# Where the FFN's output halves are summed, and when ScalarE scales the residual, in a linear-attention and FFN layer

## The chip, the cores and the metric

The kernel runs on one core of a Trainium2 chip. The metric is the device time of one execution in microseconds (us); lower is better.

## The reference

One transformer layer in fp32 on x of shape (32, 512, 256): a causal linear attention with 16 heads of 16 on the normalised x, and an FFN with quantised weights on the layer-normed result. Both add to a residual; the reference normalises twice ahead of the FFN (once outside, once inside it).

```
x = x + attn(layernorm(x))          # phi(q), phi(k) = elu+1; causal linear attention; @ Wo.T + bo
x = x + ffn(layernorm(x))           # ffn(r) = r + 0.5 * (silu(layernorm(r)*gamma+beta @ w1 + b1) @ w2 + b2)
```

So the output is x1 + layernorm(x1) + 0.5 z + 0.5 b2, where x1 is the attention's output with its residual and z the second matmul of the FFN. x1 + layernorm(x1) is x1 times a number per token plus a number per token: the kernel's `res_mul` and `res_add`.

## The kernel before

A batch is 512 tokens of 256 features: C = 4 chunks of 128 tokens, T = 2 halves of 128 features. Every engine has a program of its own, written out by hand, and engines wait for each other through counters (`Event`): `w.need(event, shift, k)` waits until the k-th count of the batch `i + shift` is there, `event.done(instruction)` counts. An engine runs its program strictly in the order written. SP issues the DMAs from one queue.

A pass `i` of the loop (`pe_iteration`, `ve_iteration`, `ac_iteration`, `po_iteration`, `sp_iteration`) works on three batches at once: the attention of batch i, the FFN of batch i-1, and the normalisation and the q and k projections of batch i+1. There are 33 passes, the first without an FFN, the last with the FFN alone.

TensorE's pass, in order: the v projection (`project_v`), transposes of k (`kt`) and of the normed x1 (`ht0`, `ht1`), 16 small matmuls for the denominators, then the first FFN matmul in eight blocks j, each in two halves `f{j}a` and `f{j}b` (`fc1(j)`, L356/L357), interleaved with the attention's scores (L400) and values (L437) of eight units u; then the transposes of the next batch's x (`ident,x_hat`, L331), q and k projections, the second FFN matmul `fc2` of chunks 0 and 1, the output projection `wo`, and `fc2` of chunks 2 and 3. Three PSUM banks go round in a ring: `f3b` takes the bank of `f2a`, and so waits until ScalarE has read `f2a` in `ffn_scaled(2)`.

ScalarE's pass (`ac_iteration`), in order: a Silu on one column, for its table (`table_warm`); four copies of v into `v_pad`, after the v projection; two copies `k_tok`; two scaled copies `gt_hi` from `ht0`, `ht1`; `ffn_scaled(0)` and `ffn_scaled(1)` (L757, they read `f0a`, `f1a`); four `res` copies (L829); `ffn_silu(0)` (L765 and L768); `ffn_scaled(2)`; then the other blocks, and at the end the exponentials of the next batch through the tile `clip` (L794, L797).

`res` is one tile of [128, 4, 256]. ScalarE writes res = x1 * res_mul + res_add into it (L829), GpSimd adds the bias (L919), VectorE adds half of `z` in two halves, in place (`final`, L644), and SP stores each half from it (`sp_store`, L965). So L829 of the next pass waits for the stores of this one:

```
w.need(res_c, -1)
w.need(store, -2)
for c in range(C):
    last = e.activation(res[:, c, :], x1[:, c, :], ACT.Identity, ...)
```

SP's pass: the load of x for batch i+2, then for each t the q and k rows of batch i+1 out to DRAM and back as stacked operands (L943 to L955), the store of half 0, the second load of x (`xb`, L938), the store of half 1.

VectorE's pass ends with `final(0)`, a scan, the sum `x1` (L713), its statistics, the normed `x_hat` (L730), `res_mul` (L732), `res_add` (L733, event `res_c`), and `final(1)`; the next pass begins with `gt_lo` (L655), which `fc1(0)` waits for.

Of the kernel before, what the change touches and what calls it, by code (L numbers as in the profile page):

```python
# [26 lines left out]
ALU = mybir.AluOpType  # L27
ACT = mybir.ActivationFunctionType
# [45 lines left out]
def build(nc, x, wq_t, bq, wk_t, bk, wv_t, bv, wo_t, bo, gamma, beta, q1, sc1, b1, q2, sc2, b2, out):  # L74
# [4 lines left out]
    C = S // P  # L79
# [13 lines left out]
    out_v = out.rearrange("b (c p) d -> b p c d", p=P)  # L93

    with ExitStack() as ctx:
        def sb(name, shape, dtype=F32):
            return ctx.enter_context(nc.sbuf_tensor(name, shape, dtype))
# [4 lines left out]
        def sem(name):  # L102
            return ctx.enter_context(nc.semaphore(name))
# [29 lines left out]
        clip = sb("clip", [P, 2, S])  # L133
# [10 lines left out]
        x1 = sb("x1", [P, C, D])  # L144
        hn2 = x_hat
        res = sb("res", [P, C, D])
# [8 lines left out]
        res_mul, res_add = sb("res_mul", [P, C]), sb("res_add", [P, C])  # L155
# [29 lines left out]
        def qk_bank(is_q, m):  # L185

            return sc[is_q] if m else ring_bank("kq"[is_q] + "0")
# [7 lines left out]
        def ring_bank(use):  # L195
            return BORROWED[use] if use in BORROWED else ring[RING[use]]


        def ev(name, per, **more):
            return Event(sem(name), per, **more)  # L200
# [35 lines left out]
        res_c = ev("res_c", 1)  # L236
        x_again = ev("x_again", 1, step=16)
        e_hn2 = ev("e_hn2", C)
        F_ = dict(early=1)
        res_m, e_res = ev("res_m", 1, **F_), ev("e_res", 1, **F_)  # L240
        ht_pe, ht_h, ht_l = ev("ht_pe", T, **F_), ev("ht_h", T, **F_), ev("ht_l", T, **F_)
        f_pe = ev("f_pe", T * FT, **F_)
        f_a, f_b = ev("f_a", FT, **F_), ev("f_b", FT, **F_)
# [1 line left out]
        z_pe, e_out = ev("z_pe", C // 2, **F_), ev("e_out", C // 2, **F_)  # L245
        store = ev("store", 2, step=16, **F_)
# [315 lines left out]
        def ve_iteration(e, i, A, Fn, N, preparation=(None, None, None)):  # L562

            w = Waiter(e, i)
# [74 lines left out]
            def final(n):  # L639

                w.need(z_pe, -1, n)
                w.need(e_res, -1)
                cs = slice(2 * n, 2 * n + 2)
                e_out.done(e.scalar_tensor_tensor(  # L644
                    out=res[:, cs, :], in0=ring_bank(f"z{n}")[:, :].rearrange("p (c d) -> p c d", c=2), scalar=0.5,
                    in1=res[:, cs, :], op0=ALU.mult, op1=ALU.add))

            if N:
                ve_norm_x(e, w, 1)
# [2 lines left out]
            if Fn:  # L652
                for t in range(T):
                    w.need(ht_h, -1, t)
                    ht_l.done(e.scalar_tensor_tensor(  # L655
                        out=gt_lo[:, t, :], in0=ring_bank(f"ht{t}")[:, :], scalar=gamma_c[:, t:t + 1],
                        in1=gt_hi[:, t, :].bitcast(F32), op0=ALU.mult, op1=ALU.subtract))
# [46 lines left out]
            if Fn:  # L704
                final(0)
            if N:
                cumulate(1, 1)
            if A:
                w.need(e_xb)
                for n in range(2):  # L710
                    w.need(wo_pe, 0, n)
                    cs = slice(2 * n, 2 * n + 2)
# [4 lines left out]
                for c in range(C):  # L717
                    last = e.bn_stats(stats2[:, c, :], x1[:, c, :])
                ln2_st.done(last)
                w.alone(ln2_st, 0)  # L720
                for c in range(C):
                    last = e.bn_aggr(mv2[:, c, :], stats2[:, c, :])
# [6 lines left out]
                for c in range(C):  # L729
# [4 lines left out]
                                                  op0=ALU.mult, op1=ALU.mult))  # L734
            if Fn:
                final(1)


        def ac_iteration(e, i, A, Fn, N):
            w = Waiter(e, i)  # L740
# [5 lines left out]
            def ffn_scaled(j):  # L746

                if not Fn:
                    return
                w.need(f_pe, -1, T * j)  # L750
                if j >= SLOTS:
                    w.need(sl, -1, j - SLOTS)
                elif A:
                    w.need(k_out[j % T], 0)
                else:
                    w.need(sl, -2)
                f_a.done(e.activation(silu_f[:, j % SLOTS, :], ring_bank(f"f{j}a")[:, :], ACT.Identity,  # L757
                                      bias=bias_1[:, j:j + 1], scale=scale_1[:, 0, j:j + 1]))

            def ffn_silu(j):  # L760
                if not Fn:
                    return
                slot = silu_f[:, j % SLOTS, :]
                w.need(f_b, -1, j)
                silu.done(e.activation(slot, slot, ACT.Silu))  # L765
                w.need(silu, -1, j)
                w.need(z_pe, -2)
                sh.done(e.activation(s_hi[:, j, :], slot, ACT.Copy))  # L768
# [15 lines left out]
            def exponentials(t, s):  # L784
                for n in (2 * t, 2 * t + 1):
                    m, is_q = n // 2, n % 2
                    w.need(qk_pe, s, n)
                    if n >= 2:
                        w.need(phi, s, n - 2)
                    else:  # L790
                        w.need(phi, s - 1)

                    part = clip[:, n % 2, :]
                    qk_clip.done(e.activation(part, qk_bank(is_q, m)[:, :], ACT.Relu,  # L794
                                              bias=bias_qkm[:, 1 - is_q, m:m + 1], scale=-1.0))
                    w.need(qk_clip, s, n)
                    qk_exp.done(e.activation(part, part, ACT.Exp, scale=-1.0))  # L797

            if Fn:
                e.activation(table_warm[:, 0:1], ones[:, 0:1], ACT.Silu)  # L800
            if A:
                for c in range(C):
                    w.need(v_pe, 0, c // 2)
                    if c == 0:
                        w.need(av_pe, -1)
                    h = c % 2
                    v_sb.done(e.activation(  # L807
                        v_pad[:, c, :, 0:4:3, :],
                        ring_bank(f"v{c // 2}")[:, h * D:(h + 1) * D].rearrange("p (r a x) -> p r a x", a=2, x=HD),
                        ACT.Copy))  # L810
            if A:
                for n in range(2):
                    w.need(kt_pe, 0, n)
                    w.need(upd_pe, -1)
                    kt_sb.done(e.activation(k_tok[:, 2 * n:2 * n + 2, :],
                                            ring_bank(f"kt{n}")[:, :].rearrange("p (c d) -> p c d", c=2), ACT.Copy))
            if Fn:
                for t in range(T):
# [3 lines left out]
                                           scale=gamma_c[:, t:t + 1]))  # L822
            ffn_scaled(0)
            ffn_scaled(1)
            if Fn:
                w.need(res_c, -1)
                w.need(store, -2)
                for c in range(C):
                    last = e.activation(res[:, c, :], x1[:, c, :], ACT.Identity, bias=res_add[:, c:c + 1],  # L829
                                        scale=res_mul[:, c:c + 1])  # L830
                res_m.done(last)
            ffn_silu(0)
            ffn_scaled(2)
            if A:
# [39 lines left out]
            if N:  # L874

                e.activation(table_warm[:, 0:1], ones[:, 0:1], ACT.Exp)  # L876
                exponentials(0, 1)
# [54 lines left out]
        def sp_load(e, w, s, batch):  # L932
            w.need(xhat, s - 1)
            load.done(e.dma_start(x_in[:, :, :], x_v[batch]))

        def sp_load_again(e, w, s, batch):
            w.need(e_x1, s - 1)
            x_again.done(e.dma_start(xb[:, :, :], x_v[batch]))  # L938

        def sp_stack(e, w, t, s):  # L940
            w.need(e_kl, s, t)
            for n, part in enumerate((k_hi, k_lo)):
                e.dma_start(k_rows[t, n], part[:, t, :]).then_inc(k_out[t].sem, 16)  # L943
            w.need(e_ql, s, t)
            for n, part in enumerate((q_hi, q_lo)):
                e.dma_start(q_rows[t, n], part[:, t, :]).then_inc(q_out[t].sem, 16)
            w.need(k_out[t], s)
            for n, part in enumerate((0, 1, 0)):
                e.dma_start(k_stack[2 * HD * n:2 * HD * (n + 1), t, :, :].bitcast(F32),
                            k_rows[t, part].rearrange("(g r) n -> r g n", g=PAIRS)).then_inc(k_in[t].sem, 16)  # L950
            w.need(q_out[t], s)
            for n, part in enumerate((0, 0, 1)):
                for odd in range(2):
                    first = HD * (2 * n + odd)
                    e.dma_start(q_stack[first:first + HD, t, :, odd, :].bitcast(F32),  # L955
                                q_rows[t, part].rearrange("(g a r) n -> a r g n", g=PAIRS, a=2)[odd])\
                        .then_inc(q_in[t].sem, 16)

        def sp_iteration(e, i, A, Fn, N, N2):
            w = Waiter(e, i)  # L960

            def sp_store(n):
                w.need(e_out, -1, n)
                cs = slice(2 * n, 2 * n + 2)
                store.done(e.dma_start(out_v[i - 1][:, cs, :], res[:, cs, :]))  # L965

            if N2:
                sp_load(e, w, 2, i + 2)
            if N:
                for t in range(T):  # L970
                    sp_stack(e, w, t, 1)
            if Fn:
                sp_store(0)
            if N:
                sp_load_again(e, w, 1, i + 1)
            if Fn:
                sp_store(1)
# [202 lines left out]
```

## Time and profile before

| | |
|---|---|
| median of 3 runs (lowest to highest) | 1870.67 us (1870.02 to 1875.25) |
| the profiled execution: its own time, its span | 1868.04 us, 1866.3 us |
| busy share: TensorE, weight loads, VectorE, ScalarE, GpSimd | 90%, 78%, 66%, 63%, 44% |
| mean granted TensorE clock | 0.935 of 2.4 GHz |
| DMA traffic | 222.86 MB, mean 119 GB/s |

The span is the stretch between the first and the last instruction of the profiled execution; the execution's own time is 1.74 us more. The busy share of TensorE counts time at either clock.

### The profile page before, as it was taken

The numbers are of one execution on the slowest core, as the hardware profiler recorded it, in microseconds if no ns is written. First come the engines' busy times: TensorE is split into PE (matmuls) and PEld (weight loads), VectorE is DVE, ScalarE is ACT, GpSimd is POOL, SyncE is SP. The second block draws the span as 40 slices with busy tenths as digits, with TensorE's granted clock in tenths as the row PEclk, the third lists the DMA queues.
The fourth block names the chain that finished last, engine by engine and source line by source line (L and its number), as shares of the span: only waits on it lengthen the run. The fifth ranks groups of instructions, "written<-read, shape, count | busy, mean of one in ns | idle before, by whom it ended". The sixth has DMA issues, their size and how long they took to land.

```text
span 1866.3 us, 39341 instructions
## 1 busy us (share of the span) xinstructions
PE 1686.4 (90%) x13860; PEld 1460.0 (78%) x13860; DVE 1240.0 (66%) x2513; ACT 1174.8 (63%) x2020; POOL 829.9 (44%) x594
## 2 busy tenths in 40 slices
PE   3998889999999888999999999998999989899987
PEld 3787778877888777888777888877878877778776
DVE  5776677666677666677666677666677666677652
ACT  2476556676665675666676665676665776566653
POOL 3254334544434544344544434544334544335543
PEclk8898999999999998999999999999999999999988
DMA  6743665334555335555334555334555334655320
GB/s 167 161 115 94 146 146 143 90 94 111 146 146 137 95 97 110 146 146 127 105 94 112 146 146 146 94 97 101 146 146 140 97 93 108 146 146 123 88 65 17
DMA packets 153937, 222.86 MB, mean 119 GB/s; under 512 B 20032, under 2 KB 71488, under 8 KB 153920
## 3 DMA queue, kind: packets, MB, share of 16 engines
q1 hardware_dynamic: 149152, 222.36, 47.4%
q10 hardware_dynamic: 4768, 0.28, 0.2%
q8 instruction: 10, 0.16, 0.0%
q14 instruction: 7, 0.06, 0.0%
HBM read 138.69 MB, written 83.89 MB: 119 GB/s over the span
## 4 chain that ended last, share of the span: by engine, by line
DMA 26%; PE 26%; ACT 14%; SPq 13%; DVE 10%; issue 9%; ACTq 1%; DVEq 0%; POOL 0%; POOLq 0%
DMA out<-res 12%; DMA k_rows<-silu_f 10%; SPq L955 8%; PE ring L301 5%; DMA q_rows<-probs 5%; PE ring L356 5%; PE sc L400 4%; PE num L437 4%; PE ring L357 3%; ACT res L829 3%; ACT silu_f L757 3%; PE ring L459 2%; DVE probs L531 2%; ACT L876 2%; ACT silu_f L765 2%
## 5 line engine op out<-in xcount | busy, mean ns | idle before, releaser
L902 POOL TENSOR_TENSOR s_lo<-silu_f,s_hi 128x512 fp32r<-128x512 f32 x256 | 340.1, 1334 | 472.8 <-ACT s_hi L768 472.8
L604 DVE SCALAR_TENSOR_TENSOR silu_f<-ring,scale,silu_f 128x512 f32<-128x512 f32 x224 | 168.3, 751 | 358.8 <-ACT silu_f L757 343.1
L356 PE MATMUL ring<-gt_hi,w_q 128*128 128x512 f32 x448 | 217.3, 485 | 109.3 <-ACT silu_f L757 109.1
L301 PE MATMUL ring<-w_hi,s_hi 128*128 128x256 f32 x1024 | 291.8, 285 | 6.4 <-POOL s_lo L902 4.9
L301 PE MATMUL ring<-w_lo,s_hi 128*128 128x256 f32 x1024 | 291.7, 285 | 0.0
L301 PE MATMUL ring<-w_hi,s_lo 128*128 128x256 f32 x1024 | 291.6, 285 | 0.0
L531 DVE TENSOR_TENSOR probs<-sc,causal 128x512 f32<-128x512 f32 x384 | 251.1, 682 | 8.8 <-PE sc L400 8.5
L356 PEld LDWEIGHTS ring<-gt_hi,w_q 128*128 128x128 f32 x448 | 92.9, 207 | 170.7 <-ACT silu_f L757 124.4
L400 PE MATMUL sc<-q_stack,k_stack 96*128 96x256 f32 x1024 | 209.0, 323 | 8.6 <-DVE probs L531 5.5
L400 PEld LDWEIGHTS sc<-q_stack,k_stack 96*128 96x128 f32 x1024 | 170.7, 212 | 44.9 <-DVE probs L531 27.8
L301 PEld LDWEIGHTS ring<-w_hi,s_hi 128*128 128x128 f32 x1024 | 198.5, 194 | 8.2 <-issue 7.0
L924 POOL TENSOR_TENSOR qk<-qk,phi_q 128x512 f32<-128x512 f32 x64 | 83.0, 1297 | 273.3 <-DVE qk L583 273.3
L301 PEld LDWEIGHTS ring<-w_lo,s_hi 128*128 128x128 f32 x1024 | 198.5, 194 | 1.2
L301 PEld LDWEIGHTS ring<-w_hi,s_lo 128*128 128x128 f32 x1024 | 198.5, 194 | 0.0
L807 ACT ACTIVATE v_pad<-state_acc 128x256 f32<-128x256 f32 x64 | 21.1, 381 | 277.4 <-PE state_acc L301 277.4
L357 PE MATMUL ring<-gt_lo,w_q 128*128 128x512 f32 x448 | 192.0, 429 | 0.0
L911 POOL TENSOR_TENSOR probs<-probs,causal 128x512 f32<-128x512 f32 x128 | 165.0, 1289 | 57.6 <-ACT probs L851 54.3
L757 ACT ACTIVATE silu_f<-ring,bias,scale 128x512 f32<-128x512 f32 x224 | 171.7, 766 | 27.0 <-PE ring L357 25.6
L437 PE MATMUL num<-probs,v_pad 128*32 128x128 f32 x4096 | 173.5, 290 | 0.4 <-DVE probs L531 0.3
L768 ACT ACTIVATE s_hi<-silu_f 128x512 fp32r<-128x512 f32 x256 | 161.8, 632 | 8.1
L765 ACT ACTIVATE silu_f<-silu_f 128x512 f32<-128x512 f32 x256 | 159.7, 624 | 0.0
L829 ACT ACTIVATE res<-x,res_add,res_mul 128x256 f32<-128x256 f32 x128 | 66.4, 589 | 112.6 <-DMA out<-res 112.6
(159 smaller groups left out, 4047.6 us busy)
## 6 DMA issues: line engine op xcount, KB each, us to landing
k_stack<-k_rows SPq DMA_DIRECT2D x192, 256.0 KB, 3.9
q_stack<-q_rows SPq DMA_DIRECT2D x384, 128.0 KB, 5.7
k_rows<-silu_f SPq DMA_DIRECT2D x128, 256.0 KB, 4.4
q_rows<-probs SPq DMA_DIRECT2D x128, 256.0 KB, 4.6
x_in<-in_x SPq DMA_DIRECT2D x32, 512.0 KB, 6.2
xb<-in_x SPq DMA_DIRECT2D x32, 512.0 KB, 7.5
out<-res SPq DMA_DIRECT2D x64, 256.0 KB, 7.1
v_pad<-in_q SPq DMA_DIRECT2D x2, 512.0 KB, 8.3
```

The source lines that it names most:

```text
L301: last = e.matmul(target, a, b, start=(n == 0), stop=(n == 3 * len(pairs) - 1))
L356: e.matmul(ring_bank(use)[:, :], w1_q[:, t, cols], gt_hi[:, t, :], start=True, stop=False)
L357: f_pe.done(e.matmul(ring_bank(use)[:, :], w1_q[:, t, cols], gt_lo[:, t, :], start=False, stop=True))
L400: last = e.matmul(sc[r][:, 2 * n * P:2 * (n + 1) * P], k_stack[:, t, pair, toks], q_stack[:, t, pair, :, toks], start=True, stop=True)
L437: last = e.matmul(num[t][32 * pair:32 * pair + 32, c * P:(c + 1) * P], v_pad[:, c, t * HT // 2 + pair, 2 * odd:2 * odd + 2, :], probs[u % ...
L531: masked[r].done(e.tensor_tensor(half_probs(u, r), sc[r][:, :].rearrange("p (h q) -> p h q", h=HV), causal[:, None, :].to_broadcast([P, HV ...
L604: f_b.done(e.scalar_tensor_tensor(out=slot, in0=ring_bank(f"f{j}b")[:, :], scalar=scale_1[:, 1, j:j + 1], in1=slot, op0=ALU.mult, op1=ALU. ...
L757: f_a.done(e.activation(silu_f[:, j % SLOTS, :], ring_bank(f"f{j}a")[:, :], ACT.Identity, bias=bias_1[:, j:j + 1], scale=scale_1[:, 0, j:j ...
L765: silu.done(e.activation(slot, slot, ACT.Silu))
L768: sh.done(e.activation(s_hi[:, j, :], slot, ACT.Copy))
L902: sl.done(e.tensor_tensor(s_lo[:, j, :], silu_f[:, j % SLOTS, :], s_hi[:, j, :].bitcast(F32), ALU.subtract))
L911: po_masked.done(e.tensor_tensor(half_probs(j, 1), half_probs(j, 1), causal[:, None, :].to_broadcast([P, HV, P]), ALU.mult))
```

## The change

`final` writes its sum to `clip`, half n to `clip[:, n, :]`, and the stores read it from there. So `final` and the first exponential of the next batch wait for the stores of the batch before, and L829 no longer does; it now needs only that `final(n)` of the batch before has read `res`. L829 becomes `residual(n)` (L807 after), two copies for each half, and moves from behind `ffn_scaled(1)` to the head of ScalarE's pass: `residual(0)` ahead of the v copies, `residual(1)` between the second and the third of them. `residual` is in the program of every pass that has an FFN.

```diff
-        res_m, e_res = ev("res_m", 1, **F_), ev("e_res", 1, **F_)
+        res_m, e_res = ev("res_m", 2, **F_), ev("e_res", 1, **F_)
...
                 w.need(z_pe, -1, n)
                 w.need(e_res, -1)
+                w.need(store, -2)
                 cs = slice(2 * n, 2 * n + 2)
                 e_out.done(e.scalar_tensor_tensor(
-                    out=res[:, cs, :], in0=ring_bank(f"z{n}")[:, :].rearrange("p (c d) -> p c d", c=2), scalar=0.5,
-                    in1=res[:, cs, :], op0=ALU.mult, op1=ALU.add))
+                    out=clip[:, n, :], in0=ring_bank(f"z{n}")[:, :], scalar=0.5,
+                    in1=res[:, cs, :].rearrange("p c d -> p (c d)"), op0=ALU.mult, op1=ALU.add))
...
                         w.need(phi, s - 1)
+                        w.need(store, s - 3)
...
+            def residual(n):
+
+                if Fn:
+                    w.need(res_c, -1)
+                    w.need(e_out, -2, n)
+                    for c in (2 * n, 2 * n + 1):
+                        last = e.activation(res[:, c, :], x1[:, c, :], ACT.Identity, bias=res_add[:, c:c + 1],
+                                            scale=res_mul[:, c:c + 1])
+                    res_m.done(last)
+
             if Fn:
                 e.activation(table_warm[:, 0:1], ones[:, 0:1], ACT.Silu)
-            if A:
-                for c in range(C):
+            residual(0)
+            for c in range(C):
+                if A:
                     w.need(v_pe, 0, c // 2)
...
+                if c == 1:
+                    residual(1)
...
             ffn_scaled(1)
-            if Fn:
-                w.need(res_c, -1)
-                w.need(store, -2)
-                for c in range(C):
-                    last = e.activation(res[:, c, :], x1[:, c, :], ACT.Identity, bias=res_add[:, c:c + 1],
-                                        scale=res_mul[:, c:c + 1])
-                res_m.done(last)
             ffn_silu(0)
...
-                store.done(e.dma_start(out_v[i - 1][:, cs, :], res[:, cs, :]))
+                store.done(e.dma_start(out_v[i - 1][:, cs, :], clip[:, n, :].rearrange("p (c d) -> p c d", c=2)))
```

The first place is ScalarE's program from the head of the loop's pass to `ffn_scaled(2)`. Before, with the events that each row waits for (`v_pe` is the v projection, `kt_pe` and `ht_pe` are the transposes, `f_pe` the first FFN matmul, `f_b` VectorE's sum of its two halves):

```order
L807 ACTIVATE v_pad<-state_acc 128x8x2x16 [waits av_pe,v_pe]
L807 ACTIVATE v_pad<-state_acc 128x8x2x16
L807 ACTIVATE v_pad<-ring 128x8x2x16 [waits v_pe]
...
L821 ACTIVATE gt_hi<-ring,gamma_c 128x512 [waits ht_pe]
L757 ACTIVATE silu_f<-num,bias,scale 128x512 [waits k_out0,f_pe]
L757 ACTIVATE silu_f<-ring,bias,scale 128x512 [waits k_out1,f_pe]
L829 ACTIVATE res<-x,res_add,res_mul 128x256 [waits store,res_c]
L829 ACTIVATE res<-x,res_add,res_mul 128x256 x3
L765 ACTIVATE silu_f<-silu_f 128x512 [waits f_b]
L768 ACTIVATE s_hi<-silu_f 128x512 [waits z_pe,silu]
L757 ACTIVATE silu_f<-ring,bias,scale 128x512 [waits f_pe]
```

The same stretch after the change:

```order
L807 ACTIVATE res<-x,res_add,res_mul 128x256 [waits e_out,res_c]
L807 ACTIVATE res<-x,res_add,res_mul 128x256
L820 ACTIVATE v_pad<-state_acc 128x8x2x16 [waits av_pe,v_pe]
L820 ACTIVATE v_pad<-state_acc 128x8x2x16
L807 ACTIVATE res<-x,res_add,res_mul 128x256 [waits e_out]
L807 ACTIVATE res<-x,res_add,res_mul 128x256
L820 ACTIVATE v_pad<-ring 128x8x2x16 [waits v_pe]
...
L758 ACTIVATE silu_f<-ring,bias,scale 128x512 [waits k_out1,f_pe]
L766 ACTIVATE silu_f<-silu_f 128x512 [waits f_b]
L769 ACTIVATE s_hi<-silu_f 128x512 [waits z_pe,silu]
L758 ACTIVATE silu_f<-ring,bias,scale 128x512 [waits f_pe]
```

The four copies and the wait for `store` have left the place between `ffn_scaled(1)` and `ffn_silu(0)`; a pair stands on either side of the first two v copies, waiting for `res_c` and `e_out`. The second place is the end of VectorE's pass, after the change, with the two `final` rows (L645), where `wo_pe` is the output projection:

```order
L71 ISA [waits e_res,z_pe]
L645 SCALAR_TENSOR_TENSOR clip<-ring,res 128x512 [waits store]
L583 SCALAR_TENSOR_TENSOR qk<-ones,phi_k 128x512 [waits phi]
L714 TENSOR_TENSOR x<-ring,xb 128x512 [waits wo_pe,e_xb]
...
L733 TENSOR_SCALAR res_mul<-ln_rstd 128x4
L734 SCALAR_TENSOR_TENSOR res_add<-mv,ln_rstd 128x4
L645 SCALAR_TENSOR_TENSOR clip<-ring,res 128x512 [waits z_pe]
```

The order there is as before; only the wait for `store` and one instruction that carries a wait are new.

## Rows read from the trace of the kernel before

**Rows 1.** The page, part 1: busy time of each engine.

```profile
PE 1686.4 (90%) x13860; PEld 1460.0 (78%) x13860; DVE 1240.0 (66%) x2513; ACT 1174.8 (63%) x2020; POOL 829.9 (44%) x594
```

**Rows 2.** Who waited for whom: us in total, times, longest us.

```profile
ACT v_pad L807 <- PE state_acc L301: 277.4, 31, 9.2
...
ACT res L829 <- DMA out<-res: 112.6, 30, 5.8
PE ring L356 <- ACT silu_f L757: 109.1, 32, 5.7
```

**Rows 3.** Timeline of ACT, one pass: start us, us, instruction [idle before, releaser].

```profile
933.76 0.66 ACT L807 ACTIVATE v_pad<-state_acc 128x256 f32<-128x256 f32 x2 [9.19 <-PE state_acc L301]
935.10 0.66 ACT L807 ACTIVATE v_pad<-ring 128x256 f32<-128x256 f32 x2 [0.69 <-PE ring L301]
...
941.09 0.78 ACT L757 ACTIVATE silu_f<-ring,bias,scale 128x512 f32<-128x512 f32 x1 [0.58 <-PE ring L357]
944.71 2.08 ACT L829 ACTIVATE res<-x,res_add,res_mul 128x256 f32<-128x256 f32 x4 [2.84 <-DMA out<-res]
946.69 0.61 ACT L765 ACTIVATE silu_f<-silu_f 128x512 f32<-128x512 f32 x1
...
947.87 0.76 ACT L757 ACTIVATE silu_f<-ring,bias,scale 128x512 f32<-128x512 f32 x1
...
969.97 0.67 ACT L794 ACTIVATE clip<-ring,bias_qkm 128x512 f32<-128x512 f32 x1
```

**Rows 4.** The chain that ended last, in the same pass.

```profile
936.65 8.03 DMA out<-res
```

**Rows 5.** Timeline of PE, the same pass.

```profile
936.65 1.85 PE L450 MATMUL state_acc<-head_one,qk 128*128 128x8 f32 x16
938.88 0.49 PE L356 MATMUL num<-gt_hi,w_q 128*128 128x512 f32 x1 [0.39 <-DVE gt_lo L655]
...
945.58 0.50 PE L356 MATMUL ring<-gt_hi,w_q 128*128 128x512 f32 x1
...
948.68 0.50 PE L356 MATMUL ring<-gt_hi,w_q 128*128 128x512 f32 x1 [2.37 <-ACT silu_f L757]
```

**Rows 6.** Stretches of the same pass; behind the busy times PEclk, DMA share, GB/s.

```profile
940.00:942.00 2.00, 2.00 (x7) 1.63 (x6) 1.28 (x4) 1.29 (x2) 0.00 (x0) 0.50 1.04 207
950.00:952.00 2.00, 2.00 (x11) 1.80 (x9) 1.35 (x4) 1.97 (x5) 1.16 (x1) 0.51 0.00 0
970.00:972.00 2.00, 2.00 (x23) 1.54 (x16) 0.66 (x1) 1.94 (x5) 2.00 (x2) 1.00 0.00 0
```

**Rows 7.** Timeline of ACT, `res` copies: the first and last between which 28 passes lie.

```profile
156.84 2.07 ACT L829 ACTIVATE res<-x,res_add,res_mul 128x256 f32<-128x256 f32 x4 [5.41 <-DMA out<-res]
...
1728.75 2.07 ACT L829 ACTIVATE res<-x,res_add,res_mul 128x256 f32<-128x256 f32 x4 [3.95 <-DMA out<-res]
```

**Rows 8.** Timeline of PE: x_hat transposes, `f0a`, `f3a`, `f4a`, `f5a`, `f6a`, x_hat transposes.

```profile
1019.19 1.09 PE L331 MATMUL ring<-ident,x_hat 128*128 128x128 f32 x8
...
1049.75 0.49 PE L356 MATMUL num<-gt_hi,w_q 128*128 128x512 f32 x1 [0.39 <-DVE gt_lo L655]
...
1055.57 0.50 PE L356 MATMUL ring<-gt_hi,w_q 128*128 128x512 f32 x1
...
1063.45 0.50 PE L356 MATMUL ring<-gt_hi,w_q 128*128 128x512 f32 x1
...
1065.86 0.50 PE L356 MATMUL ring<-gt_hi,w_q 128*128 128x512 f32 x1
...
1068.91 0.50 PE L356 MATMUL ring<-gt_hi,w_q 128*128 128x512 f32 x1
...
1073.97 1.09 PE L331 MATMUL ring<-ident,x_hat 128*128 128x128 f32 x8
```

**Rows 9.** Timeline of DVE: `res_add`, and the next pass's `final(0)`.

```profile
932.80 0.16 DVE L733 SCALAR_TENSOR_TENSOR res_add<-mv,ln_rstd 128x4 f32<-128x4 f32 x1
...
979.80 0.68 DVE L644 SCALAR_TENSOR_TENSOR res<-ring,res 128x512 f32<-128x512 f32 x1
```

## The prediction

> **What bounds the kernel now.** I began with the busy shares: TensorE is busy for 90% of the span, so it is the engine to follow, and what it does not do is at most a tenth [rows 1]. The table of waits says where that tenth goes. One line stands out: TensorE waited 109.1 us in 32 waits for `ffn_scaled` on ScalarE, and ScalarE waited 112.6 us in 30 waits for the stores from `res` ahead of the `res` copies; its 277.4 us for the v projection are idle time of an engine that is early [rows 2]. To see whether the first two are one stall, I took one pass apart. ScalarE starts `ffn_scaled(1)` at 941.09 and is done at 941.87; it stands until 944.71, when the `res` copies start (idle 2.84, released by the store); they take 2.08, `ffn_silu(0)` starts at 946.69 and `ffn_scaled(2)` at 947.87 [rows 3]. The chain of waits shows the store's 8.03 us from 936.65, so it lands at 944.68, and the chain runs through it [rows 4]. TensorE starts `f3a` at 945.58, and then stands 2.37 us until 948.68, where `f3b` gets the bank that `ffn_scaled(2)` has just read [rows 5]. It is one stall: store, `res` copies, silu, scaled, `f3b`.
>
> The stall costs more than its idle time. In this pass the granted clock is 0.51 at 950 to 952, right behind the stand, against 1.00 at 970 to 972, where TensorE is busy for 2.00 of 2.00 us [rows 6]. The lower level is 1.2 GHz, the upper 2.4.
>
> **What a pass would take without it.** The `res` copies of two passes, 28 apart, start at 156.84 and 1728.75 [rows 7]: 1571.91 / 28 = 56.14 us for a pass. A pass without the stall at the full clock I put together from pieces of one pass [rows 8]. From the x_hat transposes to `f0a`: 1049.75 - 1019.19 = 30.56. From `f0a` to `f3a`: 1055.57 - 1049.75 = 5.82. From `f3a` to `f4a` the trace has the stall in it; the step from `f5a` to `f6a` issues the same kinds of matmul, a transposed reciprocal among them: 1068.91 - 1065.86 = 3.05. From `f4a` to the next x_hat transposes: 1073.97 - 1063.45 = 10.52. Sum 49.95. So a pass has 56.14 - 49.95 = 6.19 us to lose: 109.1 / 32 = 3.41 are the wait itself, the other 2.78 the work at half clock behind it and smaller waits.
>
> **The change, part by part.**
>
> The removed wait. Without wait and copies, ScalarE can start `ffn_silu(0)` at 941.87 in that pass, and 947.87 - 946.69 = 1.18 later `ffn_scaled(2)`, which takes 0.76: done at 943.8, and by the delay below at 944.3. `f3b` can start about 0.55 behind `f3a`, at 946.1. So the ring's bank is free about 2 us before it is wanted, and the wait goes to zero, with some margin: -3.41 us. What follows is then paced by TensorE. I credit the other 2.78 us too, as the clock was low behind the stand and the stand is gone.
>
> The moved copies. `residual(0)` waits for `res_add`, which is there at 932.80 + 0.16 = 932.96 [rows 9]. Four copies took 2.08 us, a pair 1.04 to 1.1, so it ends at about 934.05, where the v copies started at 933.76: they start about 0.25 later. They need 0.54 until the next instruction can start, then `residual(1)` takes the idle 0.69 us ahead of the second v pair and more: that pair starts near 934.0 + 0.54 + 1.04 = 935.6, not 935.10 [rows 3]. That is 0.5 us. Behind it ScalarE issues `k_tok`, `gt_hi`, then VectorE `gt_lo`, and TensorE's `f0a` already waits 0.39 us for that [rows 5]; so the whole 0.5 goes to TensorE. Lower bound 1.04 - 0.69 = 0.35 (first pair wholly hidden), upper bound 2.08 (nothing hidden); I take the replay's 0.5.
>
> The head's clock. The stretch ahead of `f0a` has TensorE on 16 matmuls of 8 columns for 1.85 us and then 0.39 idle, and in this pass the clock is 0.50 at 940 to 942 [rows 5, 6]. Here `f0a` to `f3a` took 945.58 - 938.88 = 6.70, against 5.82 in the pass of rows 8: such a fall costs 0.88. It comes in some passes only; a stretch 0.5 longer should bring it in more. I take two passes in three: +0.6.
>
> The Trainium skill has a rule on this (TensorE: Matmul & The Clock Gate, Part 4: PE-mode transpose): a transpose does not count as TensorE being busy in the way a matmul does. The k and x1 transposes lie just ahead of those small matmuls, so by the page the quiet stretch is longer than the row shows, and the longer stand would bring the fall in every pass; the sum would then have 0.88 where I take 0.6. The trace agrees for the pass at 938.88 and not for the one at 1049.75.
>
> The new waits on the stores. The store landed at 944.68. The first exponential, the first to need it now, starts at 969.97 [rows 3], and `final(0)` at 979.80 [rows 9]: covers of 25 and 35 us. Pulling both 6 us forward leaves 19; if that cover were gone, each us of delay would go to the q and k chain. I cost it at nothing; the one more waiting instruction ahead of the exponential too, since TensorE is busy through and through there [rows 6]. `final` has the same size and operands, only another destination: nothing. The DMAs are the same ones at the same place of SP's queue. `residual` still comes long before GpSimd needs it.
>
> Sum for a pass: -6.19 + 0.5 + 0.6 = -5.1. The stall stands in 30 passes: -153 us. The profiled execution took 1868.04, its span 1866.3; 1868.04 - 153 = 1715. The median of the runs shown is 2.6 above that execution, so 1718.
>
> **The rivals.**
>
> A. The wait goes, the clock stays low. Other small stands inside the f-blocks or the longer stretch at the head keep TensorE at 1.2 GHz behind them. Then only 3.41 of the 6.19 come back: 3.41 - 0.5 - 0.6 = 2.3 for a pass, 69 us, 1802 for the median. For it: the clock also fell in the head, where nothing long was missing [rows 6]. Against it: from `f4a` to x_hat the pass of rows 8 ran at the full pace with the small waits it has.
>
> B. Another wait takes the place. `ffn_silu(0)` needs VectorE's sum of `f0`, which comes late by the same 0.5; the f-blocks then run as fast as ScalarE, which has two instructions more than the silus in most blocks. If `f3b` still waited for half of what it did, the pass would win 6.19 / 2 - 1.1 = 2.0: 1811. Against it: the 2 us of margin above.
>
> C. The change does nothing. That needs the store's wait not to be what `f3b` waits for, while another event comes at the same time. The chain through store, copies and silu in one piece speaks against it [rows 3 to 5]: 1871.
>
> D. Slower: `residual(0)` blocks the head of ScalarE's pass. Nothing behind it starts before `res_add`, at the end of VectorE's statistics chain. It is 0.8 us ahead of the v projection's release at 933.76 [rows 3, 9]. It turns the sign if the v copies come more than 6.19 us late, at about 940 in this pass, with `res_add` near 939; at 7 us late, 30 passes lose 0.8 each: 1895. Against it: `res_add` hangs on `x1`, whose place relative to TensorE doesn't change.
>
> **How the numbers follow.** Forecast 0.66, A or a part of it 0.19, B 0.08, C 0.03, D 0.04. Low end: no fall at the head and 0.35 for the copies, -5.84 a pass, 175 us, 1696. The forecast's own high end has the fall in every pass and a copy delay of 1 us: -4.3, 129 us, 1742. To leave out no more than 2 in 10 the range goes part of the way to A, to 1775. About 0.3% of the time, 5.6 us, is what a measurement can tell from no change; forecast, A and B all lie beyond it: faster 0.93, same 0.03, slower 0.04.
>
> **What the profile after would show.** The line of ScalarE waiting for the stores is gone, and TensorE's wait for `ffn_scaled` is below 10 us. The wait of `f0a` for `gt_lo` is near 0.9 us a pass, not 0.39. Passes are 51 us apart. The mean clock is above 0.935, about 0.97. If the passes are near 54 us with TensorE's waits gone, rival A holds. What would make the prediction wrong most easily is the clock, then a chain on ScalarE or VectorE in the head that the stall hid.

## The result, and the profile after

The change takes 1717.88 us (median of 4 runs, 1716.68 to 1719.09), the kernel before 1872.93 us on the same chip (4 runs, 1870.02 to 1875.25): ratio 0.917, 95% interval 0.915 to 0.919. The profiled execution took 1716.68 us, its span is 1715.0 us, its mean granted clock 0.969. A fall of the clock is here a stretch in which the granted clock is at the lower of its two levels, 0.50; the head of a pass is the stretch from the small matmuls to `f3a`.

From the page of the kernel after, the busy times, and the chain that ended last, by engine:

```profile
PE 1627.8 (95%) x13860; PEld 1420.3 (83%) x13860; DVE 1236.6 (72%) x2513; ACT 1173.1 (68%) x2020; POOL 830.9 (48%) x594
...
PE 51%; DVE 20%; ACT 12%; issue 11%; POOL 3%; ACTq 1%; DVEq 1%; POOLq 0%
```

That chain before the change:

```profile
DMA 26%; PE 26%; ACT 14%; SPq 13%; DVE 10%; issue 9%; ACTq 1%; DVEq 0%; POOL 0%; POOLq 0%
```

The numbers of busy instructions are the same on every engine; TensorE is busy for 95% of the span, where it was 90% [rows 1], and DMA, with 26% of the chain before, is no longer in it.

The waits after, as in [rows 2]:

```profile
ACT res L807 <- DVE res_add L734: 278.6, 32, 15.3
...
PE num L356 <- DVE gt_lo L656: 25.2, 31, 3.5
...
PEld ring L356 <- ACT silu_f L758: 3.5, 4, 1.6
...
PE ring L356 <- ACT silu_f L758: 2.0, 2, 1.1
```

ScalarE's wait for the stores is gone, and TensorE's wait for `ffn_scaled` went from 109.1 us to 2.0. The 278.6 us of the `res` copies are the idle time that the v copies had before: ScalarE is early there, now in front of another instruction. What grew is the wait of `f0a` for `gt_lo`, from 13.9 us in all to 25.2.

ScalarE's timeline in one pass, to be read beside [rows 3]:

```profile
1372.26 1.09 ACT L807 ACTIVATE res<-x,res_add,res_mul 128x256 f32<-128x256 f32 x2 [8.53 <-DVE res_add L734]
1373.26 0.63 ACT L820 ACTIVATE v_pad<-state_acc 128x256 f32<-128x256 f32 x2
1373.78 1.09 ACT L807 ACTIVATE res<-x,res_add,res_mul 128x256 f32<-128x256 f32 x2
1374.77 0.64 ACT L820 ACTIVATE v_pad<-ring 128x256 f32<-128x256 f32 x2
...
1379.37 0.78 ACT L758 ACTIVATE silu_f<-num,bias,scale 128x512 f32<-128x512 f32 x1 [1.83 <-PE num L357]
1380.21 0.78 ACT L758 ACTIVATE silu_f<-ring,bias,scale 128x512 f32<-128x512 f32 x1
1381.06 0.63 ACT L766 ACTIVATE silu_f<-silu_f 128x512 f32<-128x512 f32 x1
...
1382.27 0.76 ACT L758 ACTIVATE silu_f<-ring,bias,scale 128x512 f32<-128x512 f32 x1
```

`ffn_silu(0)` follows `ffn_scaled(1)` 0.85 us after that one started, where it was 5.60 us [rows 3]. The copies wait for `res_add`, which VectorE has at 1372.12, and the second v pair starts at 1374.77.

TensorE in the same pass: x_hat transposes, the small matmuls, `f0a`, `f3a`, `f3b`, the scores of unit 2, `f4a`, x_hat transposes:

```profile
1347.53 1.09 PE L331 MATMUL ring<-ident,x_hat 128*128 128x128 f32 x8
...
1375.95 1.85 PE L450 MATMUL state_acc<-head_one,qk 128*128 128x8 f32 x16
1378.53 0.49 PE L356 MATMUL num<-gt_hi,w_q 128*128 128x512 f32 x1 [0.73 <-DVE gt_lo L656]
...
1384.35 0.50 PE L356 MATMUL ring<-gt_hi,w_q 128*128 128x512 f32 x1
...
1384.93 0.40 PE L356 MATMUL ring<-gt_hi,w_q 128*128 128x512 f32 x1
...
1385.75 0.72 PE L400 MATMUL sc<-q_stack,k_stack 96*128 96x256 f32 x4
...
1387.42 0.50 PE L356 MATMUL ring<-gt_hi,w_q 128*128 128x512 f32 x1
...
1397.95 1.09 PE L331 MATMUL ring<-ident,x_hat 128*128 128x128 f32 x8
```

`f3b` follows `f3a` without a stand, and `f4a` comes 3.07 us after `f3a`; the prediction took 3.05 from another step. From transposes to transposes it is 1397.95 - 1347.53 = 50.42 us. The granted clock of two stretches of that pass is 1.00; in another pass it fell in the head:

```profile
866.00:868.00 2.00, 2.00 (x5) 1.61 (x6) 1.55 (x5) 0.74 (x1) 0.00 (x0) 0.50 1.08 131
...
1379.00:1381.00 2.00, 2.00 (x13) 1.70 (x12) 1.88 (x5) 1.56 (x2) 0.00 (x0) 1.00 1.06 158
1387.00:1389.00 2.00, 2.00 (x25) 1.61 (x19) 0.57 (x2) 1.95 (x4) 1.80 (x2) 1.00 0.00 0
```

Two starts of `residual(0)` between which 29 passes lie:

```profile
144.06 1.09 ACT L807 ACTIVATE res<-x,res_add,res_mul 128x256 f32<-128x256 f32 x2 [8.52 <-DVE res_add L734]
...
1627.75 1.09 ACT L807 ACTIVATE res<-x,res_add,res_mul 128x256 f32<-128x256 f32 x2 [8.44 <-DVE res_add L734]
```

A pass takes (1627.75 - 144.06) / 29 = 51.16 us, against 56.14 before [rows 7].

The mean of 29 passes, stretch by stretch, in us, read from the starts of these instructions in both traces (the first `f0a` is the one at 147.78 before and at 150.34 after):

| stretch | the prediction's piece | before | after |
|---|---|---|---|
| x_hat transposes to `f0a` | 30.56 | 30.54 | 30.99 |
| `f0a` to `f3a` | 5.82 | 6.20 | 6.58 |
| `f3a` to `f3b` | 3.05, with the next | 4.30 | 0.57 |
| `f3b` to `f4a` | | 4.49 | 2.49 |
| `f4a` to x_hat transposes | 10.52 | 10.72 | 10.52 |
| pass, `f0a` to `f0a` | 49.95 | 56.25 | 51.16 |

The pass before is 56.25 by `f0a`, 56.14 by the `res` copies, whose place in the pass shifts with the stall; the pieces are rounded.

### The profile page after: what moved, and what is told of

Its sections match the earlier page's. It is cut to its first block, busy times and chain, and to the rows that moved or that the text cites. A ratio compares the mean times of both kernels' runs of the same rounds, so it can differ in the third digit from the quotient of the medians.

```text
span 1715.0 us, 39431 instructions
## 1 busy us (share of the span) xinstructions
PE 1627.8 (95%) x13860; PEld 1420.3 (83%) x13860; DVE 1236.6 (72%) x2513; ACT 1173.1 (68%) x2020; POOL 830.9 (48%) x594
## 4 chain that ended last, share of the span: by engine, by line
PE 51%; DVE 20%; ACT 12%; issue 11%; POOL 3%; ACTq 1%; DVEq 1%; POOLq 0%
PE ring L301 17%; PE ring L356 6%; PE num L437 5%; PE sc L301 5%; PE sc L400 5%; PE ring L357 4%; DVE probs L531 4%; POOL ln_rstd L937 3%; DVE stats L719 3%; ACT v_pad L820 2%; DVE x L714 2%; ACT silu_f L758 2%; DVE x_hat L731 2%; ACT res L807 2%; PE num L356 2%
## 5 line engine op out<-in xcount | busy, mean ns | idle before, releaser
L807 ACT ACTIVATE res<-x,res_add,res_mul 128x256 f32<-128x256 f32 x128 | 69.6, 594 | 278.6 <-DVE res_add L734 278.6
L356 PE MATMUL ring<-gt_hi,w_q 128*128 128x512 f32 x448 | 206.4, 461 | 2.1 <-ACT silu_f L758 2.0
L400 PE MATMUL sc<-q_stack,k_stack 96*128 96x256 f32 x1024 | 191.0, 301 | 7.2 <-DVE probs L531 3.7
L400 PEld LDWEIGHTS sc<-q_stack,k_stack 96*128 96x128 f32 x1024 | 154.5, 192 | 43.6 <-DVE probs L531 27.4
L357 PE MATMUL ring<-gt_lo,w_q 128*128 128x512 f32 x448 | 185.5, 414 | 0.0
L437 PE MATMUL num<-probs,v_pad 128*32 128x128 f32 x4096 | 165.4, 279 | 0.5 <-DVE probs L531 0.3
L437 PEld LDWEIGHTS num<-probs,v_pad 128*32 128x32 f32 x4096 | 96.5, 109 | 31.7 <-issue 0.6
```

What stands on the lines that cost most here:

```text
L356: e.matmul(ring_bank(use)[:, :], w1_q[:, t, cols], gt_hi[:, t, :], start=True, stop=False)
L357: f_pe.done(e.matmul(ring_bank(use)[:, :], w1_q[:, t, cols], gt_lo[:, t, :], start=False, stop=True))
L400: last = e.matmul(sc[r][:, 2 * n * P:2 * (n + 1) * P], k_stack[:, t, pair, toks], q_stack[:, t, pair, :, toks], start=True, stop=True)
L437: last = e.matmul(num[t][32 * pair:32 * pair + 32, c * P:(c + 1) * P], v_pad[:, c, t * HT // 2 + pair, 2 * odd:2 * odd + 2, :], probs[u % ...
```

## The experiments

My theory was that the wait for the stores, on the path of `f3b`, is what the change removes, and that the move of the copies costs about half a microsecond a pass. The rivals: the move itself is the gain; and the clock that falls behind the stand is worth as much as the stand, or nothing. The kernel before took 1871.8 us on the chip of the first four kernels below, 1889.1 on that of the next four and 1868.7 on that of the last two; ratios are to the kernel before on the same chip. Differences from the change, 1717.88 us, can go across chips; the one kernel without the wait for the stores that ran on two chips, that with the seven copies, differs by 0.1% between them.

**The destination alone.** The copies stay where they were, without the wait:

```diff
-            residual(0)
...
-                if c == 1:
-                    residual(1)
...
             ffn_scaled(0)
             ffn_scaled(1)
+            residual(0)
+            residual(1)
             ffn_silu(0)
```

> Only the destination is changed: the sum goes to clip and is stored from there, and the four res copies stay behind ffn_scaled(1), without the wait for the stores. If the removed wait is what the change is worth (my account), the 109 us of TensorE's waits for ffn_scaled are gone to below 30; the copies' 2 us use up the margin that ScalarE has at f3b (1.8 us in the trace after), VectorE's mask for the scores of unit 2 comes up to 0.8 us late, and the head is not delayed by 0.46 a pass: 1710 to 1735 us. If the move of the copies were half of the gain, the time would be 1780 or more.

Measured 1714.1 us (1713.45 to 1715.7), ratio to before 0.916 (0.911 to 0.920). The destination alone gives all of the gain; the move adds nothing: a pass takes 51.20 us, against 51.16 in the change. TensorE's waits for ScalarE's `ffn_scaled`, for the mask and for `gt_lo`:

```profile
PEld sc L400 <- DVE probs L531: 45.1, 129, 0.8
...
PE num L356 <- DVE gt_lo L656: 14.6, 32, 1.8
...
PE ring L356 <- ACT silu_f L758: 3.0, 3, 2.2
```

and its timeline around `f3a` (971.15), `f3b`, the scores of unit 2 and `f4a` (975.20), with VectorE's sum of `f2` and the masks that these scores wait for:

```profile
971.15 0.50 PE L356 MATMUL ring<-gt_hi,w_q 128*128 128x512 f32 x1
971.73 0.44 PE L356 MATMUL ring<-gt_hi,w_q 128*128 128x512 f32 x1
973.14 1.10 PE L400 MATMUL sc<-q_stack,k_stack 96*128 96x256 f32 x4
...
975.20 0.50 PE L356 MATMUL ring<-gt_hi,w_q 128*128 128x512 f32 x1
...
971.74 0.75 DVE L604 SCALAR_TENSOR_TENSOR silu_f<-ring,scale,silu_f 128x512 f32<-128x512 f32 x1 [1.68 <-ACT silu_f L758]
972.41 1.28 DVE L531 TENSOR_TENSOR probs<-sc,causal 128x512 f32<-128x512 f32 x2
```

`f3b` doesn't wait, but the masks end only at 973.69, inside the scores, which take 1.10 us in place of 0.72, and `f3a` to `f4a` takes 4.05 us, not 3.07: with the copies there, `ffn_scaled(2)` is 2 us later, and so are VectorE's sum of `f2` and the mask behind it (and the reciprocals that TensorE transposes ahead of the scores, a wait of 0.24 us). The copies cost 0.98 us a pass at the old place and 0.44 at the new one; the old place had fewer falls of the clock (7 of 30 passes against 19, mean clock 0.982 against 0.969), and the two came out even.

**The move alone.** The sum stays in `res`, the copies go to the head with their wait:

```diff
+            def residual(n):
+
+                if Fn:
+                    w.need(res_c, -1)
+                    w.need(store, -2)
...
-                w.need(res_c, -1)
-                w.need(store, -2)
-                for c in range(C):
```

> Only the move: res copies in pairs at the head as in the change, but the sum stays in res, so each pair still waits for the stores. In the pass shown of before the stores landed at 944.7 and the v copies started at 933.8: everything from the v copies on comes some 11 to 12 us later, while the stand at f3b goes. My account gives a pass of 49.95 + 12 = 62 us and some 2045 us in all. If the place of the copies didn't matter, about 1870.

Measured 2145.0 us (2142.47 to 2150.4), ratio 1.146 (1.140 to 1.152). Direction as expected, size larger: 9.1 us a pass slower, not 5.9. The head of its pass on ScalarE:

```profile
876.37 1.09 ACT L805 ACTIVATE res<-x,res_add,res_mul 128x256 f32<-128x256 f32 x2 [21.47 <-DMA out<-res]
877.37 0.63 ACT L818 ACTIVATE v_pad<-state_acc 128x256 f32<-128x256 f32 x2
877.89 1.08 ACT L805 ACTIVATE res<-x,res_add,res_mul 128x256 f32<-128x256 f32 x2
```

TensorE waited 364.9 us in all for the v copies at the `ht` transposes. From the x_hat transposes to `f0a` its passes take 42.0 to 46.3 us, 44.3 in the mean, against 30.54, so the delay is 13.7 us rather than 11 to 12; and from `f0a` to `f3a` they take 7.1 to 7.6 us, not 5.82, with a fall in the head of every pass and a mean clock of 0.867. I had not counted this second part. So the move pays at most once the destination is changed, and is no part of the gain.

**Another place for the copies.** In the change, ScalarE stands 1.83 us ahead of `ffn_scaled(0)`. The four copies take 2.1 us:

```diff
-            residual(0)
...
-                if c == 1:
-                    residual(1)
...
+            residual(0)
+            residual(1)
             ffn_scaled(0)
             ffn_scaled(1)
```

> The change, with the four res copies between gt_hi and ffn_scaled(0), where ScalarE is idle for 1.83 us. If the copies at the head delay f0a by 0.46 us a pass and bring 19 falls of the clock in place of 11, as I read the two traces, this gives 14 us for the delay and about 10 for the falls: 1690 to 1706 us, with f0a's wait back at 0.39. If the falls at the head have nothing to do with the delay, 1703 to 1708. If the copies cost nothing where they stand, 1717.

Measured 1688.07 us (1685.53 to 1689.27), ratio 0.901 (0.896 to 0.906), 29.8 us below the change and 2 below the range that I gave. By its trace 0.45 us a pass come ahead of `f0a` (14 us) and 0.28 from `f0a` to `f3a` (8 us), with 16 falls in 30 passes in place of 19, and cheaper ones; 4.5 us more lie ahead of the loop's first `f0a` (145.80 against 150.34), which I had not counted. ScalarE's row there has no idle time left on either side, and `f0a` waits as before the change:

```profile
949.48 1.29 ACT L833 ACTIVATE gt_hi<-ring,gamma_c 128x512 fp32r<-128x512 f32 x2
950.62 2.10 ACT L807 ACTIVATE res<-x,res_add,res_mul 128x256 f32<-128x256 f32 x4
952.61 0.78 ACT L758 ACTIVATE silu_f<-num,bias,scale 128x512 f32<-128x512 f32 x1
```

**TensorE kept busy ahead of `f0a`.** Two matmuls whose result `f0a` overwrites:

```diff
+            if Fn:
+                free_bank(w, "f0a", present)
+                for _ in range(2):
+                    e.matmul(num[0][:, :], w1_q[:, 0, 0:P], w1_q[:, 0, 0:S], start=True, stop=True)
             fc1(0)
```

> The change, with two more matmuls of 512 columns into f0a's bank just before f0a, where TensorE stands 0.73 us (their result is overwritten by f0a). If the quiet stretch ahead of f0a (small matmuls and the wait) brings the falls of the clock in 19 of 30 passes, these get rarer; each costs about 1.27 us, so down to 1694 us at best. If the falls come from somewhere else, 1716 to 1720; if the added matmuls delay f0a, up to 0.2 us a pass, 1724.

Measured 1698.33 us (1693.54 to 1699.38), ratio 0.906 (0.901 to 0.911): 19.6 us below the change, with more work on the busiest engine. In the 30 passes of the loop the clock fell in the head of 19 in the change and of 4 here, and its mean rose to 0.983; `f0a` to `f3a` takes 5.99 us in the mean in place of 6.58. Where they run:

```profile
859.97 0.71 PE L487 MATMUL num<-w_q 128*128 128x512 f32 x2
860.77 0.50 PE L356 MATMUL num<-gt_hi,w_q 128*128 128x512 f32 x1
```

**Both together, and four matmuls in place of two.**

> The change, with the four res copies between gt_hi and ffn_scaled(0) and two more matmuls of 512 columns ahead of f0a. The two edits gave 30 and 20 us alone; they share the falls of the clock at the head. If the falls left in the first (88 us at half clock in its trace, 21 stretches) get rarer as in the second (58 us), 1673 to 1682 us. The wait at f0a is only 0.4 us here and the two matmuls take 0.46: if they delay f0a, 2 to 3 us are lost. If the second edit adds nothing here, 1688.

Measured 1674.52 us (1672.08 to 1676.33), the fastest kernel of this study, 43.4 us below the change. No fall of the clock is left in the loop; mean 0.987.

> As the run with two more matmuls ahead of f0a, with four, 0.9 us. They delay f0a by about 0.5 us a pass (15 us) and hold the clock up in more passes, at best the 15 us or so that the rest of the falls costs: 1680 to 1695 us. It is slower than with two unless TensorE's quiet stretch has to be filled further than the wait.

Measured 1686.16 us (1682.72 to 1687.72): 11.6 us slower than with two. There was no fall left to prevent, and the two extra matmuls, 0.43 us, delay `f0a` in 30 passes by 12.9 us in all.

**The stall put back without DMA.** Seven dependent copies between `ffn_scaled(1)` and `ffn_silu(0)` of the change:

```diff
             ffn_scaled(1)
+            if A:
+                w.need(rden, 0)
+                for m in range(7):
+                    spin.done(e.activation(qk[:, 0, :], ones[:, 0:1].to_broadcast([P, S]), ACT.Copy))
+                    w.need(spin, 0, m)
             ffn_silu(0)
```

> The change, with seven more ScalarE copies of 0.65 us (into a tile that is dead there) between ffn_scaled(1) and ffn_silu(0), 4.55 us a pass: the stall put back without DMA. With 2.0 us at that place the run with the destination alone changed lost 0.98 us a pass between f3a and f4a, because the mask for the scores of unit 2 came late; beyond that each us of delay should cost one: 3.5 us a pass, 105 in all, if the stand costs its time alone: 1823 us. If the stand also lowers the clock behind it, as I took it in the prediction, 1 to 2.8 us a pass more: 1850 to 1905 us. If only the wait at f3b counted (margin 1.8 us), 2.75 a pass: 1800.

Measured 1831.64 us (1829.99 to 1834.61), 113.8 us above the change. It lies between the two accounts and nearer the one without the clock. In its trace `f3a` to `f4a` takes 7.26 us, 4.20 more than in the change. The clock fell behind the stand in every pass and in the head in one of 30, where it did in 19 in the change, so part of the falls only changed their place.

**The kernel before, kept busy in its stand.**

```diff
+                    if use == "f3b" and A:
+                        w.need(f_b, -1, 0)
+                        for _ in range(12):
+                            e.matmul(num[1][:, :], w1_q[:, 0, 0:P], w1_q[:, 0, 0:S], start=True, stop=True)
                     free_bank(w, use, present)
```

> The kernel before, with twelve more matmuls of 512 columns between f3a and f3b, into a bank that is free there, about 2.7 us at the full clock, inside the stand of 2.4 to 6 us (their result is overwritten). The stall for the stores stays. If 2.78 of the 6.19 us a pass that I promised came back through the clock, the time falls by up to 80 us, to 1790. If the pace behind the stand is set by ScalarE's and VectorE's chain and the clock is a small part, it falls by 10 to 35 us: 1835 to 1860. If the clock doesn't matter there or isn't held up, 1868 to 1875.

Measured 1877.78 us, the median of ten runs that spread evenly from 1847 to 1904 us, against 1889.09 (1877 to 1894) for the kernel before: 11 us less. The ratio on record, 0.986 (0.981 to 0.991), is that of its four lowest runs. So I read it only as some 10 to 25 us, and not as clearly different. It is no clean test either. The mean clock rose from about 0.93 to 0.963, but it still fell behind the stand in 14 of 30 passes; and the twelve matmuls fill 3.3 us from `f3a`, where before `f3b` had started sooner in 8 of 30 passes. In its trace `f3b` to `f4a` is 3.96 us in place of 4.49, and `f3a` to `f3b` 4.68 in place of 4.30, as far as traces of two chips can be compared.

**The same test on the steady stall.** Eleven such matmuls in the kernel with the seven copies, beside that kernel again on the same chip:

> The kernel with ScalarE held up for 4.6 us a pass by seven copies (1831.6 us, TensorE stands 2.53 us at f3b, and the clock is low behind it in every pass), with eleven matmuls of 512 columns inside that stand, about 2.4 us at the full clock. A replay of its pass at the full clock has f4a 0.6 us earlier, since the mask for the scores of unit 2, at 991.1 in its trace, comes late at either clock: 18 us, 1813 us. If the clock were worth the 2.78 us a pass of the prediction, 1750. If nothing is held up, 1832.

> The same kernel without the added matmuls, on the same chip: 1830 to 1834 us, with f3a to f4a at 7.27 us.

Measured 1827.9 us (1826.34 to 1828.73) and 1833.62 us (1832.36 to 1834.79): 5.7 us of the 18 that the replay gave. The timeline of `d7_again` from `f3a` on; the gap of 2.52 ends with `f3b`, and 995.65 is `f4a`:

```profile
988.39 0.50 PE L357 MATMUL ring<-gt_hi,w_q 128*128 128x512 f32 x1
991.64 0.79 PE L357 MATMUL ring<-gt_hi,w_q 128*128 128x512 f32 x1 [2.52 <-ACT silu_f L759]
993.36 1.20 PE L401 MATMUL sc<-q_stack,k_stack 96*128 96x256 f32 x4
...
995.65 0.50 PE L357 MATMUL ring<-gt_hi,w_q 128*128 128x512 f32 x1
```

The same with the stand filled; 986.75 is `f3b`, 990.27 `f4a`:

```profile
984.07 2.70 PE L359 MATMUL num<-w_q 128*128 128x512 f32 x11
986.75 0.50 PE L361 MATMUL ring<-gt_hi,w_q 128*128 128x512 f32 x1
...
987.71 0.64 PE L464 MATMUL ring<-ident,qk 128*128 128x128 f32 x4 [0.23 <-ACT qk L854]
988.22 1.10 PE L405 MATMUL sc<-q_stack,k_stack 96*128 96x256 f32 x4
...
990.27 0.50 PE L361 MATMUL ring<-gt_hi,w_q 128*128 128x512 f32 x1
...
986.82 0.75 DVE L609 SCALAR_TENSOR_TENSOR silu_f<-ring,scale,silu_f 128x512 f32<-128x512 f32 x1 [4.42 <-ACT silu_f L763]
987.48 1.28 DVE L536 TENSOR_TENSOR probs<-sc,causal 128x512 f32<-128x512 f32 x2
```

From `f3b` to `f4a` it is 4.01 us at the low clock and 3.52 at the full one, against 2.49 in kernels without the stall. So 0.49 us a pass of what lies behind the stand is the clock's here, and 1.03 us is not: it is VectorE's sum of `f2` and the masks, which follow `ffn_scaled(2)`. They end at 988.76, and the scores that wait for them start 1.47 us behind `f3b` in place of 0.82 and take 1.10 in place of 0.72. The 0.49 would be 15 us over 30 passes; less came, because with the stand filled the clock fell in the head of 12 passes, at 7.10 - 5.82 = 1.28 us each, where without the matmuls it did in 2. That leaves 2 us, and the passes of the two traces do differ by no more, 54.71 against 54.65 us. The rest lies ahead of the loop's first `f0a`, 157.07 with the matmuls and 160.49 without.

## Why the prediction was right, and what in it was not

**The bound and the removed wait: right.** The stall was one chain, and the destination was all of it: the kernel with that edit alone reads 1714.1 us. Nothing took the wait's place: `f3a` to `f4a` is 3.06 us in the mean, 3.05 in the prediction, and in no pass did the clock fall behind it, which answers A and B.

**The pass without the stall: right.** The prediction put 49.95 us together from pieces; the sum was -6.19 + 0.5 + 0.6 = -5.1 us a pass, and 56.14 - 51.16 = 4.98 was measured. Each piece holds: 49.95 + 0.44 for the copies + 0.76 for the head's clock is 51.15. The forecast of 1715 us for the profiled execution stands against 1716.68.

**How the 6.19 us split: wrong.** The step was "3.41 are the wait itself, the other 2.78 the work at half clock behind it and smaller waits", and the credit of the 2.78 because "the clock was low behind the stand and the stand is gone". The table of stretches takes the stall apart: 4.30 - 0.57 = 3.73 us for the stand, 4.49 - 2.49 = 2.00 from `f3b` to `f4a`, 0.38 for the falls in the head of 11 passes, 0.20 behind `f4a`. Of the 2.00, 1.03 is the late mask, by the kernel with the stand filled, whose 3.52 us come back in 13 of the 16 passes of the kernel before, kept busy, in which the clock did not fall behind the stand. The other 0.97 is an estimate of the clock's part, larger than the 0.49 of the seven copies: there the clock was low for 3.1 us between `f3b` and `f4a`, here for 3.9 in the mean, and past `f4a` in 12 of 30 passes. The pass of [rows 5], from `f3b` to `f4a`:

```profile
948.68 0.50 PE L356 MATMUL ring<-gt_hi,w_q 128*128 128x512 f32 x1 [2.37 <-ACT silu_f L757]
...
950.16 1.39 PE L400 MATMUL sc<-q_stack,k_stack 96*128 96x256 f32 x4
...
953.35 0.54 PE L356 MATMUL ring<-gt_hi,w_q 128*128 128x512 f32 x1
```

The scores start 1.48 us behind `f3b` there, as with the stand filled, against 0.82 after the change. So of what the prediction gave to the clock and smaller waits, some 1.0 us a pass was a second late chain, a wait that the table of waits hardly shows for TensorE's matmuls, because it falls inside the four score matmuls. The total was safe, since it came from whole passes. With rival A, 1802 us, I priced a low clock at all of the 2.78, 83 us; the clock's whole part before, 0.97 + 0.38 + 0.20 = 1.55 us a pass, is some 47 us, so that rival's price was too high.

**The margin at `f3b`: right in number, but not the first limit.** `ffn_scaled(2)` ends at 1383.03 in the pass shown and `f3b` starts at 1384.93. But the mask's margin runs out earlier: the copies' 2 us at the old place already cost 0.98.

**The moved copies: right.** Predicted 0.5 us a pass. From the x_hat transposes to `f0a` it is 1378.53 - 1347.53 = 31.00 us after and 30.56 before: 0.44 (0.45 in the means). The wait of `f0a` was expected near 0.9 and is 0.73; the rest of the delay lies ahead of it, in the `ht` transposes, the second group of which takes the bank of the second v pair and so waits for its copies. The replay had the order of events right: `residual(0)` starts 0.14 us behind `res_add`.

**The head's clock: right in count, low in price.** Predicted two passes in three at 0.88 us; it fell in 19 of 30. From `f0a` to `f3a` a pass with a fall at its head takes 6.96 to 7.09 us, 7.04 in the mean, one without 5.82: 1.22, or 0.76 a pass in place of 0.6. The 0.88 came from the cheapest of the 11 falls before; the other ten took 6.84 to 7.00. That the quiet stretch ahead of `f0a` brings it is shown by the two added matmuls, 19 falls to 4. The prediction drew a fall in every pass from the Trainium skill's rule that a transpose does not count as TensorE being busy in the way a matmul does (TensorE: Matmul & The Clock Gate, Part 4: PE-mode transpose); the trace has 11 passes without one, and the two fastest kernels here have none in 30, with the same transposes in every pass. So the fall in every pass did not follow; the rule itself is not tested, as no run separates the transposes from the small matmuls.

**The new waits on the stores: right.** The line of ScalarE or VectorE waiting for `out<-clip` does not appear in the table of waits.

**The rivals.** D names the right place, since the copies do wait for `res_add`, but the move in that form costs 0.44 us a pass, not more than 6. The kernel with the move alone shows what happens when the head waits for something late: 9.1 us a pass.

## What to carry to other kernels

When a tile is overwritten in place and stored from there, look at who must wait for the store to land; another tile that is idle by then took the wait away here at no cost that the traces show. Instructions moved off a path should go where their engine stands anyway, and not ahead of copies that a busy engine waits for: the same four copies cost 0.98, 0.44 or about nothing a pass in three places. And to size what a stall costs, compare whole passes; the wait that a table names is only part of it, and here as much of what followed was the delay of a second chain as was the clock.

## What the runs showed of the hardware

Adding matmuls to the busiest engine made the kernel faster: two of 512 columns in a stand of 0.73 us, behind 16 matmuls of 8 columns, took 19.6 us off, because the granted clock stayed at 2.4 GHz in the head of 15 more passes. The falls also move: with a stand of 2.5 us in each pass the clock fell behind it in every pass and in the head of 1 or 2 of 30, and with that stand filled it fell in the head of 12. What a fall costs depends on what else is late: 1.22 us in the head, 0.49 behind the stand, where the mask holds the scores back at either clock. And the kernel before varied by chip and run (1861 to 1894 us), while every kernel without the wait for the stores stayed within 0.4% over its runs. In the trace of before the stand at `f3b` ranges from 1.22 to 5.65 us over the 30 passes, so the landing of the stores may be the varying part; that is not shown, and the kernel with the move alone waited for them too and stayed within 0.4%.
